# Three buffers for turned units and high halves, with the low halves written over the turned units

## The reference

```python
A = adj + jnp.eye(adj.shape[0], dtype=adj.dtype)
d_inv_sqrt = jax.lax.rsqrt(jnp.sum(A, axis=1))
A_hat = A * d_inv_sqrt[:, None] * d_inv_sqrt[None, :]
x = layernorm(x + elu((A_hat @ x) @ w))          # layer 0
x = layernorm(x + relu((adj @ x) @ W.T + b))     # layer 1
```

## Time and profile before

| | |
|---|---|
| time, median of 3 runs | 867.38 us (866.87 to 867.91) |
| profiled execution | 869.26 us, its span 867.3 us |
| granted clock of the matrix engine, mean | 0.972 |
| busy: PE / DVE / ACT / GpSimd | 792.3 / 745.5 / 511.8 / 190.6 us |
| instructions | 10759 |
| read from HBM, written | 176.82 MB, 4.19 MB |

### The profile page before, as it was taken

How to read it: one execution, slowest core, us unless ns; L and a number is a source line. 1 busy time by engine, 2 the same in 40 slices (tenths; PEclk the granted TensorE clock), 3 DMA queues, 4 the chain that set the end, 5 groups by cost and what they waited for, 6 DMA issues and landing times.

```text
span 867.3 us, 10759 instructions
## 1 busy us (share of the span) xinstructions
PE 792.3 (91%) x3532; PEld 652.6 (75%) x3532; DVE 745.5 (86%) x587; ACT 511.8 (59%) x1132; POOL 190.6 (22%) x181
## 2 busy tenths in 40 slices
PE   0465989799999999999999999999999999999996
PEld 0344768578888888888888888888888888888884
DVE  2368979999889999889998999899898998887962
ACT  1355666566776674578776746576744656446351
POOL 0004353351453600012221001020202223023031
PEclk9977989899999999999999999999999999999998
DMA  9999999789999699799989988898997898997400
GB/s 269 320 320 284 216 172 227 180 205 238 254 269 287 144 216 222 210 201 224 212 215 240 208 217 190 188 226 189 211 271 169 205 225 191 213 220 182 102 24 25
DMA packets 183590, 181.71 MB, mean 210 GB/s; under 512 B 6768, under 2 KB 183536, under 8 KB 183536
## 3 DMA queue, kind: packets, MB, share of 16 engines
q1 hardware_dynamic: 94704, 93.21, 46.0%
q10 hardware_dynamic: 88832, 87.83, 42.9%
HBM read 176.82 MB, written 4.19 MB: 209 GB/s over the span
## 4 chain that ended last, share of the span: by engine, by line
PE 62%; DVE 1%; ACT 0%; issue 0%; POOLq 0%; POOL 0%; ACTq 0%; DVEq 0%
PE acc L992 19%; PE acc L994 19%; PE acc L993 19%; PE proj L948 3%; PE proj L946 1%; PE proj L927 0%; ACT acc L481 0%; DVE turned L644 0%; PE acc L969 0%; DVE stats L854 0%; DVE raw L848 0%; PE acc L1025 0%; ACT a_hi L471 0%; DVE v_lo L699 0%; ACT normed L628 0%
## 5 line engine op out<-in xcount | busy, mean ns | idle before, releaser
L992 PE MATMUL acc<-a_hi,v_hi 128*128 128x512 f32 x1024 | 408.9, 399 | 20.5 <-DVE a_lo L659 11.0
L471 ACT ACTIVATE a_hi<-turned 128x1024 fp32r<-128x1024 f32 x256 | 264.4, 1058 | 264.0 <-PE acc L994 134.8
L993 PE MATMUL acc<-a_lo,v_hi 128*128 128x512 f32 x1024 | 403.7, 394 | 0.0
L994 PE MATMUL acc<-a_hi,v_lo 128*128 128x512 f32 x1024 | 403.6, 394 | 0.0
L659 DVE TENSOR_TENSOR a_lo<-turned,a_hi 128x1024 fp32r<-128x1024 f32 x256 | 321.1, 1291 | 32.5 <-ACT a_hi L471 23.4
L644 DVE STREAM_TRANSPOSE turned<-raw 128x2048 f32<-128x2048 f32 x122 | 280.0, 2302 | 6.1
L992 PEld LDWEIGHTS acc<-a_hi,v_hi 128*128 128x128 f32 x1024 | 195.5, 191 | 64.1 <-issue 13.5
L994 PEld LDWEIGHTS acc<-a_hi,v_lo 128*128 128x128 f32 x1024 | 195.3, 191 | 41.6
L993 PEld LDWEIGHTS acc<-a_lo,v_hi 128*128 128x128 f32 x1024 | 195.6, 191 | 40.2
L481 ACT ACTIVATE acc<-raw 128x256 f32<-128x256 f32 x198 | 73.0, 369 | 20.6 <-DMA raw<-in_adj_dram 11.7
L666 DVE TENSOR_REDUCE deg_parts<-raw 128x4 f32<-128x1024 f32 (+3 forms) x29 | 43.0, 1483 | 21.3 <-DMA raw<-in_adj_dram 21.3
(11 more groups left out here) (69 smaller groups left out, 408.2 us busy)
## 6 DMA issues: line engine op xcount, KB each, us to landing
raw<-in_adj_dram SPq DMA_DIRECT2D x154, 512.0 KB, 9.1
raw<-in_adj_dram ACTq DMA_DIRECT2D x154, 512.0 KB, 9.8
x_row<-in_x_dram SPq DMA_DIRECT2D x64, 128.0 KB, 5.4
out_dram<-normed ACTq DMA_DIRECT2D x28, 128.0 KB, 3.3
held<-in_adj_dram ACTq DMA_DIRECT2D x4, 512.0 KB, 13.0
held<-in_adj_dram SPq DMA_DIRECT2D x4, 512.0 KB, 13.0
partial<-in_adj_dram ACTq DMA_DIRECT2D x2, 512.0 KB, 19.0
partial<-in_adj_dram SPq DMA_DIRECT2D x2, 512.0 KB, 18.4
```

What stands on the lines that cost most here:

```text
L471: nc.scalar.activation(a_hi[u % 2][:, part, :], turned[u % 2][:, part, :], ACT.Copy).then_inc(s_hi, 1)
L992: pe.matmul(dst, v_hi[:, k, ch], a_hi[u % 2][:, t, :], start=begin, stop=False)
L993: pe.matmul(dst, v_hi[:, k, ch], a_lo[u % 2][:, t, :], start=False, stop=False)
L994: ins = pe.matmul(dst, v_lo[:, k, ch], a_hi[u % 2][:, t, :], start=False, stop=end)
```

## The change

Three turned units and three sets of high halves take the place of two and two. The low halves have no buffers of their own any more: `a_lo[i]` is a second name, of type fp32r, for the bytes of `turned[i]`, and `lo(u)` writes its result over its own input. The number of tiles of this size in memory is six before and after. The waits follow from that. A buffer may be turned into when PE has used the unit that was there three units ago. The high halves wait for PE's use of the unit three back. The low halves wait only for the high ones.

```diff
+    TURNS = 3
-        turned = [sb(f"turned{i}", [P, GT, GN]) for i in range(2)]
-        a_hi = [sb(f"a_hi{i}", [P, GT, GN], F32R) for i in range(2)]
-        a_lo = [sb(f"a_lo{i}", [P, GT, GN], F32R) for i in range(2)]
+        turned_at = -(-nc.sbuf_base // B32) * B32
+        turned = [sb(f"turned{i}", [P, GT, GN]) for i in range(TURNS)]
+        a_hi = [sb(f"a_hi{i}", [P, GT, GN], F32R) for i in range(TURNS)]
+        a_lo = [nc.alloc_sbuf_tensor_at(f"a_lo{i}", [P, GT, GN], F32R, offset=turned_at + 4 * GT * GN * i) for i in range(TURNS)]
...
                 act.wait_ge(s_turn, u + 1)
                 for half, part in HALVES:
-                    if u >= 2:
-                        act.wait_ge(s_used, halves_of(u - 2, half))
-                        act.wait_ge(s_lo, halves_of(u - 2, half))
-                    nc.scalar.activation(a_hi[u % 2][:, part, :], turned[u % 2][:, part, :],
+                    if u >= TURNS:
+                        act.wait_ge(s_used, halves_of(u - TURNS, half))
+                    nc.scalar.activation(a_hi[u % TURNS][:, part, :], turned[u % TURNS][:, part, :],
                                          ACT.Copy).then_inc(s_hi, 1)
...
-                if u >= 2:
-                    dve.wait_ge(s_hi, halves_of(u - 2, 1))
-                    dve.wait_ge(s_lo, halves_of(u - 2, 1))
+                if u >= TURNS:
+                    dve.wait_ge(s_used, halves_of(u - TURNS, 1))
...
                 for half, part in HALVES:
                     dve.wait_ge(s_hi, halves_of(u, half))
-                    if u >= 2:
-                        dve.wait_ge(s_used, halves_of(u - 2, half))
-                    nc.vector.tensor_tensor(a_lo[u % 2][:, part, :], turned[u % 2][:, part, :],
-                                            a_hi[u % 2][:, part, :].bitcast(F32),
+                    nc.vector.tensor_tensor(a_lo[u % TURNS][:, part, :], turned[u % TURNS][:, part, :],
+                                            a_hi[u % TURNS][:, part, :].bitcast(F32),
                                             ALU.subtract).then_inc(s_lo, 1)
```

More of the change, by code:

```diff
@@ L637, in turn @@
                 name, row, col, n, _ = units[u]
-                if u >= 2:
-                    dve.wait_ge(s_hi, halves_of(u - 2, 1))
-                    dve.wait_ge(s_lo, halves_of(u - 2, 1))
+                if u >= TURNS:
+                    dve.wait_ge(s_used, halves_of(u - TURNS, 1))
                 own = accs[units[u][4]][2] == 0 and row == col
                 src = raw[buffer_of[n]][:].rearrange("p b (t h c) -> p h t b c", h=2, c=B32)[:, col % 2]
-                dst = turned[u % 2][:].rearrange("p t (b r) -> p t b r", r=B32)
+                dst = turned[u % TURNS][:].rearrange("p t (b r) -> p t b r", r=B32)
                 ins = nc.vector.transpose(dst, src)
@@ L648, in turn @@
                     dve.wait_ge(s_block, row + 1)
-                    diag = diagonal_of(turned[u % 2])
+                    diag = diagonal_of(turned[u % TURNS])
                     nc.vector.tensor_tensor(diag, diag, ident4, ALU.add).then_inc(s_turn, 1)
@@ L991, in product @@
                         end = u == last and t == GT - 1
-                        pe.matmul(dst, v_hi[:, k, ch], a_hi[u % 2][:, t, :], start=begin, stop=False)
-                        pe.matmul(dst, v_hi[:, k, ch], a_lo[u % 2][:, t, :], start=False, stop=False)
-                        ins = pe.matmul(dst, v_lo[:, k, ch], a_hi[u % 2][:, t, :], start=False, stop=end)
+                        pe.matmul(dst, v_hi[:, k, ch], a_hi[u % TURNS][:, t, :], start=begin, stop=False)
+                        pe.matmul(dst, v_hi[:, k, ch], a_lo[u % TURNS][:, t, :], start=False, stop=False)
+                        ins = pe.matmul(dst, v_lo[:, k, ch], a_hi[u % TURNS][:, t, :], start=False, stop=end)
                     if t % 2:
```

## The result

The changed kernel takes 871.79 us (median of 9 runs, 869.07 to 874.06), the kernel before 866.87 us (9 runs, 864.54 to 868.86): a ratio of 1.0057, with a 95% interval of 1.0038 to 1.0076. It is slower by 0.6%, or 4.9 us. The profiled execution has a span of 870.5 us, against 867.3.

The account below looks back on a forecast made before the run. PE, working without a pause from unit 12 on, was taken as the bound. Terms 0 + 0.6 + 0.7, some 1.3 to 1.4 us, on the timed median of 867.4 gave 868.8 us, range 866.0 to 873.0.

Parts of the forecast that it names:

- The likeliest case: Whole kernel: time within the forecast's own range of 866.4 to 870.0 us, no measurable change; same had 0.51.
- A: From 370 us on, low halves blocked by GpSimd additions reach PE: 873 us, or 883 with all 15; chance 0.20.
- B: At 8 rows, v_lo's whole wait plus row work exceeds the fixed reserve: 4.5 us lost, 872 us; chance 0.18.
- held row work: Where row work meets held transposes, PE loses 0.2 us at each of three places: 0.6 us.
- 0.7 for GpSimd: After 370 us, low halves stretched beside GpSimd's 15 additions reach PE in three cases, some 0.5 us each, half taken.
- The reserve: Behind a held transpose, the first low half is ready a fixed 1.85 us before PE wants it.
- The transposes' wait: At L644, transposes would wait for PE for some 20 to 40 us in all.
- The start of unit 13: At 172.7 us; a move of over 1 us would show the forecast wrong and point to C.
- C: In the first 165 us, freed ACT shortens the chain: faster, 2 us would give 865.4; chance 0.10.
- PE's waits on a_lo in the view: After 165 us, they would grow by 1 to 2 us in pieces under 1 us; over 3 us meant wrong.
- the walk at units 75 to 79: Tracing of row work behind held transposes in these units: PE loses 0 to 0.2 us.
- three such places: Places where row work meets held transposes, including the first held ones in the degree part: 0.2 us charged at each.

Follow-up runs that it names:

- the first two experiments: Kernel before plus only the transpose's wait for unit u-3: 871.28 us; changed kernel with four turned units and two sets of high halves: 866.28 us.
- two buffers in place: Changed kernel with two turned units and two sets of high halves instead of three, transposes waiting for unit u-2: 1415.24 us in one run.
- the late wait: Kernel before with the transpose's wait for unit u-3 added from unit 95 on only: 870.37 us, ratio 1.0045.
- the small addition: Changed kernel with GpSimd's layer 1 residual addition of v_hi and v_lo cut to 4 values of one tile: 868.77 us.
- four turned units: Changed kernel with four turned units and two sets of high halves; transposes wait for u-4, high halves for u-2: 866.28 us.
- both with transposes in halves: Changed kernel with each transpose cut into two, each half waiting for its own half of u-3: 866.68 us; also with residual in two units: 867.00 us.

## Why the prediction was right or wrong

The forecast was 868.8 us and no measurable change. The measured 871.8 is slower, clear of noise, inside the range of 866 to 873, and on the side that had 0.40. The likeliest case was the wrong one. That the range holds 871.8 is in part luck: its upper part came from rivals A and B, whose prices of about 5 us each rested on things that did not happen as told (a third to half of 15 additions, a whole wait of v_lo in each of 8 rows). The sum had 0.6 us for held row work and 0.7 for GpSimd. The traces have 0.74 + 1.45 us and 2.4.

**Right: the bound and the kind of cost.** PE has no pause after unit 12, so the regained waits of DVE and ACT brought nothing. The in-place write costs nothing that can be measured. The transpose's wait accounts for the whole loss, as the first two experiments show. The reserve was put at 1.85 us. In the trace after it is 1.7 to 1.8 us in most units of phase B without row work (units 42, 43, 46, 54, 61, 71 and more), where it had been 2.2 to 4.8 us. The waits moved as forecast: high halves to under 3 us (1.6), the high halves' releaser from PE towards DVE. The transposes' wait was put at 20 to 40 us and is 56.4, a miss. I had counted 23.4 and 13.5 us of idle time given up; the low halves gave up 30.7, v_lo 12.1, DVE's busy time fell by 7.7 and the span grew by 3.2, which makes 53.7.

**Two signs that told little.** The start of unit 13 moves by 2.4 us, to an earlier time, which was to be the sign of C. It is 1.1 to 4.6 us earlier in the traces of all the other kernels too (two buffers in place left out), and 3.1 in that of the late wait, which is the kernel before up to there. So the sign cannot tell C from what varies anyway, and the time, which is longer, speaks against C. PE's waits on a_lo in the view were to grow by 1 to 2 us after 165 us. Over the whole run they grow from 11.0 to 12.1, but after 165 us they fall from 4.4 to 1.3, as a wait of 4.3 us now lies ahead of 165. Only the starts show the 2.4 us.

**Right: the walk at units 75 to 79.** The first half of unit 75 was put 0.1 to 1.0 us ahead of PE and is 1.0 ahead, unit 76's -0.2 to 0.7 and is 0.8, unit 77's 1.6 and is 1.8. PE loses nothing there.

**Wrong: the step that took this place for all of them.** "I charge 0.2 at each of three such places" rests on a walk in phase B, where a unit carries at most one piece of about 1.2 us besides the aggregation. The list of row work in the part on the bound names L738, L749 and L717, and leaves out the residual of layer 1, whose two pieces (L754 and L758, 2.45 us) come in one unit in phase C. A walk there would have found 0.3 us of reserve (unit 107). Rival B named the point from which it decides, 2.7 us of row work, and sought it at the wrong place, at v_lo in phase B: v_lo's wait went from 13.5 to 1.4 us, and where it is made to come back it costs 0.7 at one row.

**Wrong: collisions priced as chance.** The term of 0.7 us took GpSimd's additions as falling anywhere in a unit, one in five or six on a half that matters. They are tied to the same row: the residual delays the low halves, the moments wait for the residual, and GpSimd's addition stands behind the statistics of those moments in its queue, so it falls into the unit after. So the two fall together in the four longest rows of phase C that have a residual, and cost 2.4 us as four steps of 0.6. In a shorter row the pair at 688.85 is stretched to the same 3.95 us and no step follows. Rivals A and B were priced apart, and what happened is their product. Each experiment that removes one of them removes the four steps.

**Not foreseen: who else waits for the vector engine.** At unit 97 PE does not wait for low halves but for the first piece of the residual, which frees `proj` for the next projection. The transpose ahead of it is held by 3.22 us:

```profile
658.92 2.31 DVE L644 STREAM_TRANSPOSE turned<-raw 128x2048 f32<-128x2048 f32 x1 [3.22 <-PE acc L992]
661.16 2.32 DVE L657 TENSOR_TENSOR a_lo<-turned,a_hi 128x1024 fp32r<-128x1024 f32 x2
663.39 1.22 DVE L752 TENSOR_TENSOR raw<-proj,b_sb 128x1024 f32<-128x1024 f32 x1
```

```profile
664.76 3.69 PE L946 MATMUL proj<-wt_sb,raw 128*128 128x256 f32 x16 [0.50 <-DVE raw L752]
```

And the transpose of unit 34, held in the degree part of the program, ends in a wait of the fold of the degrees ahead of unit 37:

```profile
323.15 0.25 PE L904 MATMUL acc<-deg_sums,fold 128*32 128x4 f32 x8 [1.54 <-DVE deg_sums L682]
```

I had followed the low halves behind a held transpose and had set all else down to "row work". Both are instructions of DVE for which PE waits. They cost 0.74 and 0.5 to 1.5 us. The second was among the three places that the prediction charged with 0.2 us. Its size varies from trace to trace: it is 0.54 us with the small addition, an edit of layer 1 alone, and there a pair of low halves on the way takes 3.36 us that takes 4.27 in the trace of the change. Without the held transpose it is gone (-0.1 with four turned units and with the late wait).

The sum of what the starts show from unit 24 on is 3.0 + 1.2 = 4.2 us. The medians differ by 4.9 us with an interval of 3.3 to 6.6, so the two agree.

## What to carry to other kernels

When a buffer's release moves from a late consumer to the one at the head of an in-order queue, the reserve of everything behind it becomes a fixed number. Work it out once, then hold against it the heaviest unit in every phase, with all pieces that fall into it, and what another engine does at that moment, not a typical unit. Cutting the held instruction in two, each waiting for its own half, gave the loss back with the same memory, and so did moving one tile from the high halves, which didn't need it, to the turned units, which did. Neither is faster than the kernel before: with PE already at work without a pause, there was nothing for the third buffer to win.

## What the runs showed of the hardware

A low half (two inputs in SBUF) that meets GpSimd's addition is stopped until the addition ends: at 732.68 the pair took 3.95 us for 2.3, and GpSimd ended 1.74 us after it began. In the Trainium skill, SBUF — State Buffer, section "Who interferes with whom", a vector instruction with two SBUF inputs contends with a GpSimd instruction that reads SBUF, and whichever issues second is blocked until the first is done. These rows agree.

The last unit takes 6.95 to 6.98 us from its first matmul to its last in six of the twelve traces (before, four turned and two high, both with transposes in halves, wait late, two buffers in place) and 5.36 us in the other six (the change among them). In the trace of before a part of it runs at the 1.2 GHz level: the granted clock is 0.50 from 849.9 to 853.1 us, and 1.00 in the same unit of the change. It follows the same eight short matmuls (L969 before) in all, no edit touches it, and why the clock falls in some and not in others stays open. The profile of the change has 1.6 us less there than that of before, so that its span is only 3.2 us longer although its unit 127 starts 5.0 us later.
